# Where a tile's key rows are gathered from: a joined key-and-V' table, or key itself

## The reference

```python
q = x @ Wq.T + bq
k = key @ Wk.T + bk
v = value @ Wv.T + bv
scores = q @ k.T / N ** 0.5
s = scores * adj                          # adj: 4096 x 4096, of 0 and 1, sparse
s = where(abs(s) < 1e-5, -1e9, s)
out = softmax(s, axis=-1) @ v @ Wm.T + bm
y = layernorm(x + out)                    # over the 512 features, eps 1e-5
```

## Time and profile before

| | us |
|---|---|
| median of 3 runs (lowest, highest) | 565.24 (560.36, 566.16) |
| profiled execution, its own time | 560.05 |
| span of the profiled execution | 558.2 |
| TensorE busy, share of the span | 510.8 (92%) |
| VectorE busy | 337.4 (60%) |
| ScalarE busy | 229.7 (41%) |
| GpSimd busy | 232.0 (42%) |
| mean granted TensorE clock | 0.973 of full speed |

### The profile page before, as it was taken

The page is one execution under the profiler, slowest core; times in us unless marked ns, Lnnn a source line. Parts: engine busy times, 40 slices in busy tenths (PEclk is TensorE's granted clock), DMA queues, the critical chain, the costliest instruction groups (busy, mean ns, idle before and its releaser), DMA issues.

```text
span 558.2 us, 5679 instructions
## 1 busy us (share of the span) xinstructions
PE 510.8 (92%) x1678; PEld 267.3 (48%) x1678; DVE 337.4 (60%) x756; ACT 229.7 (41%) x463; POOL 232.0 (42%) x205
## 2 busy tenths in 40 slices
PE   6999999999389974999999989999999999999983
PEld 3444444444134443556555545555555555555651
DVE  1574678976961047678688888765645543453552
ACT  0233123333123222334552554464373464465473
POOL 3000020008600366466675565655664565466400
PEclk9999999999879996999999999999999999999996
DMA  9999999999999999595899899656547455346422
GB/s 350 423 406 426 426 422 387 384 397 418 408 395 356 340 418 389 175 360 206 320 383 408 318 292 354 217 162 212 164 150 242 105 182 187 99 144 227 114 76 79
DMA packets 43957, 160.81 MB, mean 288 GB/s; under 512 B 9874, under 2 KB 9874, under 8 KB 37778
## 3 DMA queue, kind: packets, MB, share of 16 engines
q1 hardware_dynamic: 20690, 102.21, 47.0%
q0 software_dynamic: 16992, 38.26, 22.3%
q10 hardware_dynamic: 6240, 19.92, 9.0%
HBM read 161.98 MB, written 25.17 MB: 335 GB/s over the span
## 4 chain that ended last, share of the span: by engine, by line
PE 43%; DMA 22%; DVE 19%; SPq 8%; ACT 4%; issue 3%; POOL 0%; ACTq 0%; DVEq 0%; POOLq 0%
DMA big<-adj_tiles 16%; PE bank L496 13%; PE bank L602 11%; PE bank L622 10%; SPq L353 7%; DVE big L898 7%; PE bank L578 5%; DMA table<-key 4%; DMA kv<-table,index 2%; PE bank L612 1%; DVE big L933 1%; DVE slots L931 1%; PE bank L593 1%; DVE big L901 1%; DVE score L1035 1%
## 5 line engine op out<-in xcount | busy, mean ns | idle before, releaser
L392 POOL DMA_INDIRECT kv<-table,index x90 | 100.1, 1112 | 111.5 <-PE bank L622 89.2
L487 PE MATMUL bank<-kv,big 128*128 128x512 f32 x256 | 113.6, 604 | 10.6 <-DMA big<-valueT 10.6
L496 PE MATMUL bank<-big,M 128*128 128x512 f32 x256 | 120.0, 596 | 0.0
L421 POOL DMA_INDIRECT adj_g<-adj_cols,index x96 | 107.8, 1123 | 29.3 <-issue 29.3
L898 DVE TENSOR_TENSOR big<-big 128x2048 bf16<-128x2048 f32 x32 | 73.2, 2288 | 41.3 <-DMA big<-adj_tiles 41.3
L602 PE MATMUL bank<-keyT,qT 128*128 128x384 f32 x256 | 88.9, 490 | 6.2 <-issue 4.9
L622 PE MATMUL bank<-kv,probT 128*128 128x512 f32 x192 | 89.7, 604 | 0.9 <-ACT probT L809 0.6
L487 PEld LDWEIGHTS bank<-kv,big 128*128 128x128 f32 x256 | 49.1, 193 | 72.6 <-issue 61.0
L602 PEld LDWEIGHTS bank<-keyT,qT 128*128 128x128 f32 x256 | 47.6, 190 | 46.7 <-issue 19.1
L496 PEld LDWEIGHTS bank<-big,M 128*128 128x128 f32 x256 | 44.6, 192 | 34.2 <-issue 34.2
L1030 DVE SCALAR_TENSOR_TENSOR score<-bank,c_cols,adjT 128x384 f32<-128x384 f32 x32 | 19.8, 618 | 67.8 <-PE bank L602 66.4
(11 more groups left out here) (99 smaller groups left out, 522.4 us busy)
## 6 DMA issues: line engine op xcount, KB each, us to landing
big<-adj_tiles SPq DMA_DIRECT2D x32, 2048.0 KB, 11.3
big<-valueT ACTq DMA_DIRECT2D x8, 1024.0 KB, 13.4
x_buf<-x SPq DMA_DIRECT2D x32, 256.0 KB, 4.5
table<-key SPq DMA_DIRECT2D x8, 1024.0 KB, 22.8
out<-y_buf SPq DMA_DIRECT2D x32, 256.0 KB, 3.7
big<-xT SPq DMA_DIRECT2D x6, 1024.0 KB, 12.0
table<-qT ACTq DMA_DIRECT2D x4, 1024.0 KB, 20.9
table<-y_buf ACTq DMA_DIRECT2D x4, 1024.0 KB, 28.5
```

The source lines that it names most:

```text
L392: pool.indirect_dma_start(kv[:, b, c, :], None, table, bass.IndirectOffsetOnAxis(index[:, t, c:c + 1], 0), bounds_check=N - 1, oob_is_err= ...
L421: pool.indirect_dma_start(adj_g[:, b, c, :], None, adj_cols, bass.IndirectOffsetOnAxis(index[:, t, CH + c:CH + c + 1], 0),).then_inc(adj_g ...
L487: mm = nc.tensor.matmul(bank[4 + t % 2][:, :], col_buf[nb % 2][:, d, k * P:(k + 1) * P], G[:, d, :], start=(d == 0), stop=(d == DC - 1))
L496: mm = nc.tensor.matmul(ps[:, :], M[:, d, a * P:(a + 1) * P], col_buf[nb % 2][:, d, :], start=(d == 0), stop=(d == DC - 1))
```

## The change

The table in DRAM holds only V', 2 KB a row. The eight copies of key into it and the semaphore behind them are gone. Every tile, not only tiles 0 and 1, gathers its keys from key and its V' rows from the table, with the same index: nine gathers for a tile instead of six. The keys of tile t wait for the transposes of tile t-4 (`keyT_ps`), the V' rows for values(t-4) as before. The order on POOL for t >= 4 is keys, adj columns, V' rows. The index of half rows is gone, with three short VectorE instructions. `values(t)` on TensorE now waits for the V' gathers of its own tile each time.

```diff
@@ sync
-            for nb in range(NB):
-                sp.dma_start(table[nb * 512:(nb + 1) * 512, 0:D], key[nb * 512:(nb + 1) * 512, :]).then_inc(table_in, 16)
@@ gpsimd
-            def gather(t):
+            def gather_keys(t):
                 b = t % KV
                 if t % BT == 0:
                     pool.wait_ge(index_ready, (t // BT + 1) * (2 * CH))
                 if t >= KV:
+                    pool.wait_ge(keyT_ps, CH * (t - KV + 1))
+                for c in range(CH):
+                    pool.indirect_dma_start(
+                        kv[:, b, c, 0:D], None, key,
+                        bass.IndirectOffsetOnAxis(index[:, t, c:c + 1], 0),
+                        bounds_check=N - 1, oob_is_err=False,
+                    ).then_inc(gathered[b], 16)
+
+            def gather_values(t):
+                b = t % KV
+                if t >= KV:
                     pool.wait_ge(pv_ps, t - KV + 1)
                 for c in range(CH):
                     pool.indirect_dma_start(
-                        kv[:, b, c, :], None, table,
+                        kv[:, b, c, D:2 * D], None, table,
                         bass.IndirectOffsetOnAxis(index[:, t, c:c + 1], 0),
                         bounds_check=N - 1, oob_is_err=False,
-                    ).then_inc(gathered[b], 16)
-                if t >= KV:
-                    gather_adj(t)
+                    ).then_inc(v_gathered[b], 16)
...
-            pool.wait_ge(half_ready, CH)
             for t in range(EARLY):
                 gather_values(t)
             nc.gpsimd.memset(kv_flat[:, kv_half:kv_half + 2048], 0.0).then_inc(kv_zeroed, 1)
             pool.wait_ge(kv_zeroed, 3)
-            pool.wait_ge(table_in, 16 * NB)
             for t in range(EARLY, T):
-                gather(t)
+                gather_keys(t)
+                if t >= KV:
+                    gather_adj(t)
+                gather_values(t)
@@ tensor
             def values(t):
                 pe.wait_ge(probT_sb, t + 1)
-                if t < EARLY:
-                    pe.wait_ge(v_gathered[t], 16 * CH)
+                pe.wait_ge(v_gathered[t % KV], (t // KV + 1) * (16 * CH))
@@ scalar
-                    act.dma_start(table_blocks[nb][:, :, D:2 * D], v_out[slot]).then_inc(v_stored[slot], 16)
+                    act.dma_start(table_blocks[nb], v_out[slot]).then_inc(v_stored[slot], 16)
@@ vector, index_slots
-                    if b == 0:
-                        nc.vector.tensor_scalar(half_index[:, :, c], v[:, 0:EARLY], -2.0 * G8, cst[:, C_BV:C_BV + 1],
-                                                ALU.mult, ALU.add).then_inc(half_ready, 1)
@@ kernel
-    table = nc.dram_tensor("table", (N, 2 * D), F32).ap()
+    table = nc.dram_tensor("table", (N, D), F32).ap()
```

More of the change, by code:

```diff
@@ L51 @@
 C_TWO = C_B + 3 * DC
-C_BV = C_TWO + 1
-C_GRP2 = C_BV + 1
+C_GRP2 = C_TWO + 1
 C_ALL = C_GRP2 + P
@@ L82, in build @@
         index = sb("index", [P, T, 2 * CH], I32)
-        half_index = sb("half_index", [P, EARLY, CH], I32)
         c_cols = sb("c_cols", [P, T])
@@ L160, in build @@
         cols_in = [sem(f"cols_in{i}") for i in range(2)]
-        table_in = sem("table_in")
         x_in = [sem(f"x_in{i}") for i in range(XB)]
@@ L164, in build @@
         gathered = [sem(f"gathered{i}") for i in range(KV)]
-        v_gathered = [sem(f"v_gathered{i}") for i in range(EARLY)]
+        v_gathered = [sem(f"v_gathered{i}") for i in range(KV)]
         stored = [sem(f"stored{i}") for i in range(YB)]
@@ L194, in build @@
         index_ready = sem("index_ready")
-        half_ready = sem("half_ready")
         lead_sb = sem("lead_sb")
@@ L468, in _ @@
                                 pool.indirect_dma_start(
-                                    kv[:, 0, c, :], None, table,
+                                    kv[:, 0, c, 0:D], None, key,
+                                    bass.IndirectOffsetOnAxis(index_now[:, c:c + 1], 0),
+                                    bounds_check=N - 1, oob_is_err=False,
+                                ).then_inc(g_kv_in, 16)
+                                pool.indirect_dma_start(
+                                    kv[:, 0, c, D:2 * D], None, table,
                                     bass.IndirectOffsetOnAxis(index_now[:, c:c + 1], 0),
@@ L511, in spread_slots @@
                     pe.wait_ge(index_ready, b * (2 * CH))
-                if b == 1:
-                    pe.wait_ge(half_ready, CH)
                 for c in range(CH):
@@ L679, in _ @@
                             it = block_no * 4 + j
-                            wait_apart(pe, g_kv_in, it * (16 * CH) + 16 * CH)
+                            wait_apart(pe, g_kv_in, it * (32 * CH) + 32 * CH)
                             for c in range(CH):
@@ L1228, in layout @@
     const[:, C_EPS] = 1e-5
-    const[:, C_BV] = 2 * const[:, C_BK] + 1
     const[:, C_TWO] = 2.0 * (p % G8 == G8 - 1)
```

## The result

The changed kernel takes 642.35 us (median of four runs, 639.5 to 649.38) against 562.8 for the kernel before (four runs, 558.92 to 566.16): 1.141 times as long, interval 1.131 to 1.151. The forecast was 584, with 595 as its upper end. The sign was right, the size was not: 79.6 us were lost where 21 to 24 had been forecast, and some 58 us are missing from the sum. The profiled execution is the longest of the four, 649.38 us, span 647.5.

A forecast was written before the change was run, and what follows sets the result against it. POOL's gather issue was to bound the loop: first V' gather 182.9, tile 4 issued by 216.4, 27 tiles of 11.6 us plus 29 us of stalls, then the tail, span 583.1; 584 us forecast, range 566 to 595.

The forecast's parts named there:

- the start: Up to tile 2: without the copy of key, POOL's first V' gather comes 5.8 us earlier and TensorE gains 8.6 us.
- the shorter bound: Last V' store before POOL's first gather: 10.1 us, the shortest store seen under adj load, taken within 7 to 15.9.
- the sum for TensorE alone: Whole kernel if only TensorE held it: span 549.6 after gaining 8.6 us, plus 1.9 outside, 551.5 us.
- the price of a gather: POOL's main loop: 1.00 us and a 0.30 gap per key or V' gather, whatever the row size; 11.6 us a tile.
- the first rival: Main loop: POOL is hidden and gets faster, TensorE alone decides at 551.5 us, needing a gather cycle under 1.17 us; chance 0.09.
- the stalls, and that they multiply: POOL's gathers in the main loop, slowed by VectorE's instructions: 29 us together, between 19 and 36.
- the stalls do not multiply: POOL's main loop: gathers slip past VectorE's instructions, 555 us without stalls, 565 with a third of them; chance 0.09.
- the sum along POOL: From first V' gather at 182.9 through 27 tiles of 11.6 us, stalls and tail: span 583.1, 585 us, taken as 584.
- from there TensorE waits for POOL in every iteration: Main loop from near tile 11: POOL's lead of some 14 us is used up at about 2 us a tile.
- Worse than summed: Last V' store gains nothing (+5.8) and stalls at the upper end (+7), 597 us, or late landings lengthen waits; chance 0.10.

The follow-up runs named there:

- e3: The changed kernel, but the key gathers of tile t wait for values(t-4) in place of the key transposes of tile t-4; 586.09 us, ratio 1.046.
- e4: The changed kernel without the V' gathers of tiles 4 to 31 (old rows used), six gathers a tile; 545.89 us, ratio 0.975.
- e17: The kernel before with three more plain transfers of adj columns a tile, issued by POOL, into an unread buffer; 561.4 us, ratio 0.999.
- e8: The kernel before with one more wait ahead of each tile's gathers, for the key transposes of tile t-4; 562.29 us, ratio 1.000.
- e18: The kernel before with two memsets of 128 x 2048 a tile on GpSimd and no further transfer; 589.8 us, ratio 1.053.
- e14: The kernel before with three more plain transfers of adj columns a tile, issued by SyncE, into an unread buffer; 562.31 us, ratio 1.004.
- e19: The kernel before with three more plain transfers of adj columns a tile from SyncE, a word-for-word repeat of e14; 562.51 us, ratio 1.004.
- e7: The changed kernel, but the key gathers of tile t wait for the adj transposes of tile t-4 in place of the key transposes; 639.35 us, ratio 1.135.
- e2: The kernel before with three more gathers of adj columns a tile from tile 2 on, nine in all, into unread buffers; 588.12 us, ratio 1.050.
- e12: The kernel before with three more unread gathers of adj columns a tile, e2 word for word in another set; 645.26 us.

## Why the prediction was wrong

**Right: the start.** Forecast were POOL's first V' gather at 182.9, the main loop at 193.0 and keys of tile 2 at 208.1. The changed kernel had 182.44, 192.61 and 207.73, right behind values(0):

```profile
205.16 2.74 PE L612 MATMUL bank<-kv,probT 128*128 128x512 f32 x6
207.73 1.47 PE L569 MATMUL bank<-cst,kv 128*128 128x128 f32 x12
```

That the moment fits to 0.5 us is two small misses that cancel. The last V' store was issued at 173.28, 1.25 us later than before, and it took some 8.4 us, counted to 0.8 us ahead of the first gather (8.7 is the shortest landing in e3), less than the 10.1 of the shorter bound. e4 shows the gain in the time: 545.9, where the sum for TensorE alone gave 551.5. The 5.6 us between them are for the most part a term that the forecast put at nothing, the clock. Before, TensorE came out of its wait of 8.32 us at half its clock (granted 0.50 from 216 to 219 us):

```profile
216.69 2.82 PE L578 MATMUL bank<-cst,kv 128*128 128x128 f32 x12 [8.32 <-DMA kv<-table,index]
219.31 0.85 PE L593 MATMUL bank<-cst,adj_g 128*128 128x128 f32 x3
219.95 2.45 PE L496 MATMUL bank<-big,M 128*128 128x512 f32 x4
```

The same three groups take 1.47, 0.49 and 1.88 us in e4 and in the changed kernel. values(1) starts 11.1 us earlier in the changed kernel (215.72 against 226.86) and 12.1 in e4, not 8.6; values(31) takes 4.54 us before, at a granted 0.66, and 2.84 in e4, at 1.00.

**Right: the price of a gather.** 1.00 and a gap of 0.30, with 2 KB rows as with 4 KB. One figure beside it is wrong: 33 us over 270 gathers are 0.12 each, so the first rival needed a cycle under 1.27 us, not 1.17. The Trainium skill (DMA: Bandwidth & Descriptors, Anatomy of one DMA) calls descriptor generation small, and by it the three gathers would be hidden. Measured, they cost 586.1 - 545.9 = 40 us where the traces are complete, against 584 - 551.5 = 32.5 in the sum, in which TensorE's own part was 5.6 us too large (e4 also moves fewer bytes, so not all of the 40 need be issue time); here the measurement decides against the page.

**Right: the stalls, and that they multiply.** 29 us were forecast, e3 shows 28.9, and its halves fit too: 21.7 up to tile 14 where 23 were forecast, 7.3 behind it where 6 were. The rival "the stalls do not multiply" fell with it. The Trainium skill (SBUF — State Buffer, Who interferes with whom) infers that descriptor generation isn't held by a two-input tensor operation; e3's key gathers have a mean of 1176 ns where the undisturbed one takes 1003, and the earlier trace rows has one such pair. In e3 twelve gathers were slowed beside VectorE's L888 and ended 0.82 to 0.88 us behind it, 16.8 us of excess together. For indirect gathers the trace doesn't agree. POOL's plain transfers in e17 show nothing of it: all 90 took 562 to 709 ns, the two that met that reduction among them. So it need not be the writing of descriptors that is held; that an indirect gather also reads its indices from SBUF is an argument for the difference, not shown.

**Right: the sum along POOL, where the traces are complete.** Adj of tile 31 was to start its last gather at 557.6 and land at 561.2; in e3 it starts at 557.55 and the transposes start at 561.09. Span 583.1 forecast, 582.6 measured. TensorE's waits there name what was forecast, gathers of adj and of keys, if 19 times and not in every iteration:

```profile
PE bank L584 <- DMA adj_g<-adj_cols,index: 21.5, 13, 3.1
PE bank L569 <- DMA kv<-key,index: 10.2, 6, 3.4
```

**Wrong: "from there TensorE waits for POOL in every iteration".** This step made POOL's time the time of the loop, and put nothing beside it for TensorE's own signals. In the changed kernel TensorE waits for ScalarE's keyT, ScalarE for a signal that comes late, and POOL for TensorE. Up to values(13) the two traces are level, 363.80 in the changed kernel and 364.68 in e3:

```profile
364.68 2.84 PE L612 MATMUL bank<-kv,probT 128*128 128x512 f32 x6
...
375.34 2.74 PE L612 MATMUL bank<-kv,probT 128*128 128x512 f32 x6
```

From there to values(14) e3 takes 10.7 us and the changed kernel 45.4: 34.8 us in one iteration. From values(14) to the end it is 207.3 against 238.3: 31.0 more. With the 0.9 of lead this is the whole difference of the spans, 647.5 - 582.6 = 64.9. The stretch around that iteration in both traces, the changed kernel's first (us, then busy time of PE, its weight loads, DVE, ACT, POOL, then granted clock, DMA share and GB/s):

```profile
345.00:400.00 55.00, 28.29 (x98) 15.23 (x98) 19.62 (x47) 12.83 (x24) 42.71 (x41) 0.81 0.49 141
```

```profile
345.00:400.00 55.00, 51.63 (x194) 29.31 (x195) 29.70 (x75) 26.16 (x50) 42.81 (x41) 0.97 0.56 165
```

POOL does the same 41 gathers in both; TensorE does half the work. The clock falls to 0.81 after TensorE has stood still, and so makes the loss larger; it isn't its start, because the keys were transposed at full clock and the copies were late all the same. The DMA engines carry less than in e3, so bandwidth isn't it.

Of the rivals none named a late signal. "Worse than summed", at 597, had the right sign but other grounds, and its ground was wrong: stores gained what was forecast and stalls were as summed. Could the forecast have had it? The trace of before shows not one late signal, and e8 shows none in a kernel with six gathers where records are missing. What the forecast could have kept is a wider upper end for a resource (POOL's queue) driven to a load that the trace of before doesn't contain.

**What stays open.** Shown: late signals come with eight or nine gathers a tile, whatever they gather and whatever they wait for, and only where records are missing; six gathers didn't bring them there (e8), and a POOL that is busy by other work brought two, of 1.4 and 1.1 us (e18), one trace each. Not shown: why, and what that condition is. Missing records and late signals may be two effects of one cause, or the recording of the semaphores may itself hold TensorE's signals back, in which case part of these 60 us would be the price of being profiled; every time here comes from profiled executions, so no run tells this apart. Whether plain transfers would bring them too was asked twice (e14, e19) and both times the trace was complete. The changed kernel itself never ran with a complete trace; that it would take about 586 there is inferred from e3. Either way it is slower than before: by 4 to 5% at best, by 14% as measured.

## What to carry to other kernels

Count what an engine issues, not only what it moves: a split gather costs its issue time twice, and 1.3 us times nine against TensorE's 11 us an iteration was enough to lose, 15.5 us gained without the V' gathers (e4) and 40 given back. When the profile after names "another core or an unknown queue" on one core, look whether the producer had finished long before; if so, and if landing times are missing from the page, run the same text again in another set before you build theories on single edits. A comparison holds only within its set: e3 at 586 beside e7 at 639 looked like a finding about a wait, and was none.

## What the runs showed of the hardware that I had not expected

- A signal from TensorE to ScalarE can arrive 35 us after the matmuls ended (367.95 to 403.31), while TensorE goes on with other work; one behind the other, its signals come 5.6 to 10.6 us apart.
- The same text took 588 us in one set and 645 in another (e2, e12), with the kernel before at 561.4 and 559.3 beside it: a condition that six gathers don't feel and nine do.
- GpSimd's issue of a plain 64 KB transfer takes 0.59 us, about half of an indirect gather of the same rows (1.0 us); three a tile were free (e17).

```profile
L408 POOL DMA_DIRECT2D extra<-adj_cols x90 | 51.0, 590 | 0.1
```
